# Early-fusion layer: the tokenizer's last wave in another order, with the mixer's first gated products between its norms

## The chip, the cores and the metric

The kernel runs on one core of one Trainium2 chip. The metric is the time of one execution on the device in microseconds (us), as the median of three runs.

## What is computed

Three parts follow one another on a batch of 32 images. The tokenizer makes 49 tokens of 192 channels from each image; a row for the class and 32 text rows are added, which gives 82 rows an image. Then come a Mamba mixer with a selective scan and a feed-forward part, and last attention with a mixture of eight experts. The change touches the end of the tokenizer and the start of the mixer:

```python
h = relu(dwconv(h, f1_dw, f1_pw, f1_pwb))
h = relu(dwconv(h, f2_dw, f2_pw, f2_pwb))
h = dwconv(loc + h, f3_dw, f3_pw, f3_pwb)          # 3x3 taps per channel, then a 1x1 product
t = (t - mu) / sqrt(var + 1e-05) * ln_g + ln_b     # over the 192 channels of each token
h = concatenate([cls_tok, t]), then the text rows
# mixer, for rounds of 4 images
z = (rmsnorm(layernorm(h)) @ W_in.T) * sigmoid(... @ W_gate.T)
xdbl = z @ W_xproj.T                                # dt_in, B, C
h_t = exp(dt * A) * h_{t-1} + dt * z * B            # the scan, 16 states
```

## The kernel before

**The tokenizer** (`tokenizer`) works on four chunks (CH) of eight images (IM) and runs them through a pipeline of seven waves (WAVES, w = 0 to 6). Each engine has its instructions in an order written out by hand, and semaphores join them. Chunk c goes through the convolutions in wave c, the first fusion layer (tile PF[0], DF[0]) in wave c+1, the second (PF[1], DF[1]) in wave c+2 and the third (PF[2], DF[2]) in wave c+3. The nine taps of a depthwise layer are shared: for one half of the channels VectorE multiplies and adds them (`dw`, L174 and L176, one input and the running sum in PSUM bank 3, the last tap writes DF); for the other half ScalarE weighs them (`weigh`, L344) and GpSimd adds them (`add_up`, L492).

The last 1x1 product turns the channels to the free side: TensorE makes for each two images one product in a bank of PSUM (L300; four matmuls of 192 columns, each recorded as two passes), four such for each chunk. VectorE adds the bias while it copies them to T0 (`take_rows`, L414, which raises s_t0), makes statistics of the rows (L420, L423), GpSimd makes the root (`roots`, L479 and L481), and VectorE norms the rows (`norm_rows`: eight scalings, L429, and two operations on all, L432 and L434, which raises s_t1). SyncE then stores the chunk to H, and loads weights of the mixer between the stores.

Since DF[2] is there once, the taps of a chunk wait for the products of the chunk before (s_f[2]). Since three banks are there for the products, product n waits for the add of product n-3 (s_t0). In the last wave VectorE's order is: norms of chunk 1, adds and statistics of chunk 2, taps of chunk 3, adds and statistics of chunk 3, norms of chunk 2, norms of chunk 3.

**The mixer** (`mamba`) works in eight rounds (ROUNDS) of four images, each with 16 turns, one for each state. What a round needs ahead of its scan is made in the round before it, by `pre(j, par, s, other)` of each engine. For round 0 these pieces are made in the tokenizer's last waves, at named points, where `tok` calls back `tail(point)` of the mixer: s = 0 is the scaled input hn (ScalarE, L899), s = 2 the transposes (TensorE L764, ScalarE L904), s = 3, 4, 5 the three tiles of gate and input products (TensorE L784, tanh on ScalarE L909, z on VectorE L1030), s = 6 the projection to dt, B and C (TensorE L792; ScalarE L913 to L916 copy it; VectorE takes the residual R, L1035). Two banks of PSUM (SIDE) are shared by these pieces in turn, so the products of a tile wait for z of the tile before. From there ScalarE makes softplus, which gives dt (VectorE L1038 to L1045 in round 0).

At its last but one tail VectorE halves the gate weights (L1105) and spreads the one-hot rows to sel (L1106); both raise s_cst. After the tokenizer VectorE makes `chunk_stats` of chunks 1 to 3 (L1014 to L1021), from which GpSimd makes roots (L1133, L1135), then P (L1141) and Bx (L1173), which the first scan of VectorE (L1082) needs.

Of the kernel before, what the change touches and what calls it, by code (L numbers as in the profile page):

```python
# [93 lines left out]
def tokenizer(nc, ctx, at, ps, H, vec, ident, eye, xcol, w_pl, w_pg, had, pw_mix, w96, vecs, pwb_row, lng_row, lnb_row, cls_row, txt):  # L94


    if True:
# [37 lines left out]
        f3_bank = [psC[0:PATCHES, 0, 0:2 * D], psC[0:PATCHES, 1, 0:2 * D], psC[0:PATCHES, 2, 0:2 * D]]  # L135
# [73 lines left out]
        def tensor(pe, tail):  # L209
# [32 lines left out]
            for w in range(WAVES):  # L242
# [46 lines left out]
                if 0 <= w - 3 < CH:  # L289
# [5 lines left out]
                    for n in range(c * IM // 2, (c + 1) * IM // 2):  # L295
                        if n >= 3:
                            pe.wait_ge(s_t0, n - 2)
                        for j in range(2):
                            for k in range(2):
                                mm = pe.matmul(f3_bank[n % 3][:, j * D:(j + 1) * D], dense(DF[2], k)[:, 2 * n + j - c * IM, :],  # L300
                                               wf[:, 3, k, :], start=k == 0, stop=k == 1)
                        mm.then_inc(s_f[2], 1)

        def scalar(act, tail):
# [42 lines left out]
            for w in range(WAVES):  # L347
                if w + 1 < CH:
                    gelu(w + 1)
                if w == WAVES - 1:  # L350
                    tail("last wave")
# [48 lines left out]
        def vector(v, tail):  # L400
# [9 lines left out]
            def take_rows(c):  # L410

                for n in range(c * IM // 2, (c + 1) * IM // 2):
                    v.wait_ge(s_f[2], n + 1)
                    v.tensor_tensor(T0[:, 2 * n:2 * n + 2, :], f3_bank[n % 3].rearrange("p (j c) -> p j c", j=2),  # L414
# [22 lines left out]
            for w in range(WAVES):  # L437
# [5 lines left out]
                if 0 <= w - 1 < CH:  # L443
# [3 lines left out]
                    dw(v, own, PF[0], DF[0], (0,), w - 1, V_F_DW, s_dwf[0])  # L447
                if 0 <= w - 5:
# [3 lines left out]
                if w == WAVES - 1:  # L452
                    tail("last taps")
# [7 lines left out]
                if 0 <= w - 3 < CH:  # L461
# [5 lines left out]
            take_rows(CH - 1)  # L467
            norm_rows(CH - 2)
            tail("last rows")
            norm_rows(CH - 1)  # L470
# [133 lines left out]
def mamba(nc, ctx, block, at, ps, tok, H, vec, ident, w_zg, w_x, w_dt, a_log, w_o, w_ug, w_dn, onehot, b_d, xs):  # L604
# [4 lines left out]
    if True:  # L609
# [13 lines left out]
        s_w = sem("b_w"); s_wA = sem("b_wA"); s_wo = sem("b_wo"); s_wug = sem("b_wug"); s_cst = sem("b_cst"); s_zero = sem("b_zs"); s_zf = sem("b_zf")  # L623
# [118 lines left out]
        def _(pe):  # L742
# [101 lines left out]
            def first():  # L844
                pe.wait_ge(tok.s_t0, CH * IM // 2)
                pe.sem_inc(s_left, 1)
                pe.wait_ge(s_cst, 3)
# [21 lines left out]
            EARLY = (2, 3, 4)  # L869
# [9 lines left out]
        def _(act):  # L879
# [6 lines left out]
            def softplus_in(j, m):  # L886
                if isinstance(j, int) and j == 0 and m == 0:
                    act.wait_ge(s_cst, 2)
# [89 lines left out]
            def first():  # L978
# [6 lines left out]
                act.wait_ge(s_cst, 3)  # L985
# [10 lines left out]
            def tail(point):  # L996
                pre(0, 0, 0, None)
# [5 lines left out]
        def _(v):  # L1003
# [96 lines left out]
            def tail(point):  # L1100
                if point == "last but one taps":
                    v.wait_ge(tok.s_cls, 32)
                    chunk_stats(0)
                    v.wait_ge(s_w, 64)
                    v.tensor_scalar(wzg[:, :, 0, :], wzg[:, :, 0, :], 0.5, None, ALU.mult).then_inc(s_cst, 1)  # L1105
                    v.tensor_copy(sel[:], oh[:, STATE:2 * STATE].rearrange("p (s a) -> p s a", a=1).broadcast_to([HD, STATE, 128])).then_inc(s_cst, 1)  # L1106
                if point == "last wave":
                    v.wait_ge(tok.s_lr, CH)
                    pre(0, 0, 3, None)
                if point == "last taps":  # L1110
# [994 lines left out]
```

## Time and profile before

| | us |
|---|---|
| median of 3 runs (lowest, highest) | 1568.92 (1567.16, 1569.36) |
| the profiled execution | 1572.95 |
| its span | 1571.1 |

The profile is of one execution. Engines are called PE (TensorE), PEld (its weight loads), DVE (VectorE), ACT (ScalarE), POOL (GpSimd) and SP or SPq (SyncE); DVEq is VectorE's queue, without a data instruction. A timeline has a line for each run of equal instructions: its start, how long it took in all, the instruction, and in square brackets how long the engine stood idle ahead of it and who released it. L numbers are lines of the kernel.

### The profile page before, as it was taken

The numbers are of one execution on the slowest core, as the hardware profiler recorded it, in microseconds if no ns is written. First come the engines' busy times: TensorE is split into PE (matmuls) and PEld (weight loads), VectorE is DVE, ScalarE is ACT, GpSimd is POOL, SyncE is SP. The second block draws the span as 40 slices with busy tenths as digits, with TensorE's granted clock in tenths as the row PEclk, the third lists the DMA queues.
The fourth block names the chain that finished last, engine by engine and source line by source line (L and its number), as shares of the span: only waits on it lengthen the run. The fifth ranks groups of instructions, "written<-read, shape, count | busy, mean of one in ns | idle before, by whom it ended". The sixth has DMA issues, their size and how long they took to land. (4 is left out here: it accounts for less than half of the span.)

```text
span 1571.1 us, 19634 instructions
## 1 busy us (share of the span) xinstructions
PE 1263.1 (80%) x5818; PEld 832.9 (53%) x5819; DVE 1044.7 (66%) x1955; ACT 708.8 (45%) x1486; POOL 755.3 (48%) x493
## 2 busy tenths in 40 slices
PE   6796736388898989889878589888888439999996
PEld 4342323144554555545435368777777417777775
DVE  3699787899888978989895437766667503333332
ACT  1147522576757758585752055444442112222221
POOL 2028963668758675776771501144444622222222
PEclk9696667699999999999999789999897569999999
DMA  5100000530403304040300111112100122222221
GB/s 158 52 1 0 27 9 26 164 129 1 129 17 113 103 26 129 0 129 6 123 1 0 36 54 40 54 53 67 51 22 22 29 55 35 37 37 37 34 36 23
DMA packets 71417, 81.02 MB, mean 52 GB/s; under 512 B 13390, under 2 KB 63205, under 8 KB 71257
## 3 DMA queue, kind: packets, MB, share of 16 engines
q1 hardware_dynamic: 52066, 68.63, 14.0%
q0 software_dynamic: 17152, 9.24, 4.3%
q10 hardware_dynamic: 2136, 2.37, 0.5%
q8 instruction: 32, 0.52, 0.1%
q14 instruction: 31, 0.25, 0.1%
HBM read 48.86 MB, written 30.01 MB: 50 GB/s over the span
## 5 line engine op out<-in xcount | busy, mean ns | idle before, releaser
L1173 POOL TENSOR_TENSOR Bx<-dtz,Bb 128x984 f32<-128x984 f32 x128 | 288.2, 2270 | 54.3 <-DVE hs L1082 54.3
L1082 DVE TENSOR_TENSOR_SCAN hs<-ps,Bx 128x492 f32<-128x492 f32 x256 | 287.6, 1164 | 30.4 <-ACT ps L973 25.4
L973 ACT ACTIVATE ps<-dt,A 128x324 f32<-128x324 f32 (+1 forms) x512 | 214.1, 454 | 106.5 <-DVE hs L1082 104.9
L856 PE MATMUL ps<-hs,b_id 128*128 128x492 f32 x512 | 243.3, 598 | 9.2 <-DVE y L1050 9.1
L1937 POOL DMA_INDIRECT out<-yt,dest x48 | 74.4, 1549 | 219.9 <-DVE yt L1924 214.7
L1092 DVE TENSOR_TENSOR hs<-hs,ps 128x984 f32<-128x984 f32 x128 | 150.2, 1174 | 2.6
L1818 PE MATMUL e_ps<-W,xT 97*128 (+1 forms) x384 | 138.3, 503 | 1.5 <-ACT xT L1872 1.0
L856 PEld LDWEIGHTS ps<-hs,b_id 128*128 128x128 f32 x512 | 94.4, 198 | 84.5 <-issue 82.3
L1910 DVE COPY hT_<-e_ps 128x768 f32<-128x768 f32 x48 | 46.0, 958 | 129.0 <-PE e_ps L1827 128.7
L1722 POOL TENSOR_TENSOR c_x<-c_x,bro 82x192 f32<-82x192 f32 x32 | 19.7, 616 | 195.2 <-DVE c_x L1565 194.7
L1837 PE MATMUL e_ps<-W,hT_ 128*128 x576 | 109.2, 327 | 0.8 <-DVE yb L1918 0.8
L1878 ACT ACTIVATE hb<-e_ps 128x768 f32<-128x768 f32 x48 | 38.9, 811 | 144.1 <-PE e_ps L1818 144.1
L823 PE MATMUL ps<-hfT,wug 96*128 96x328 f32 x256 | 83.7, 472 | 24.8 <-DVE av L1067 24.1
L1713 POOL DMA_INDIRECT buckets<-XS,c_slot x64 | 91.1, 1424 | 24.9 <-issue 19.1
L1818 PEld LDWEIGHTS e_ps<-W,xT 97*128 97x128 f32 (+1 forms) x384 | 69.9, 192 | 55.0 <-issue 17.0
L1837 PEld LDWEIGHTS e_ps<-W,hT_ 128*128 128x128 f32 x576 | 91.4, 190 | 1.4 <-issue 1.4
L492 POOL TENSOR_TENSOR DF<-DF,prod 96x441 f32<-96x441 f32 x84 | 87.5, 1042 | 6.6
L841 PE MATMUL ps<-P,sel 96*128 96x328 bf16 x128 | 40.2, 316 | 54.8 <-DVE hs L1092 41.0
L823 PEld LDWEIGHTS ps<-hfT,wug 96*128 96x128 f32 x256 | 49.1, 199 | 64.0 <-DVE av L1067 40.7
L1419 PEld LDWEIGHTS c_ps<-V,PT 82*82 82x82 f32 x768 | 69.3, 169 | 13.8 <-issue 7.6
L1872 ACT ACTIVATE xT<-e_ps,m_vec 96x128 f32<-96x128 f32 x96 | 38.4, 448 | 81.5 <-PE e_ps L1808 81.5
L1532 DVE TENSOR_REDUCE mx<-c_ps 82x12 f32<-82x984 f32 x32 | 37.7, 1177 | 51.7 <-PE c_ps L1406 51.4
(247 smaller groups left out, 2446.4 us busy)
## 6 DMA issues: line engine op xcount, KB each, us to landing
Bb<-b_rows SPq DMA_DIRECT2D x32, 656.0 KB, 6.6
buckets<-b_zero SPq DMA_DIRECT2D x8, 2288.0 KB, 15.4
xg<-buckets SPq DMA_DIRECT2D x48, 104.0 KB, 1.9
xc<-in_xcol SPq DMA_DIRECT2D x4, 1176.0 KB, 9.4
W<-in_w1d SPq DMA_DIRECT2D x8, 582.0 KB
W<-in_w2d SPq DMA_DIRECT2D x8, 576.0 KB
out<-H SPq DMA_DIRECT2D x8, 246.0 KB
H<-P SPq DMA_DIRECT2D x4, 294.0 KB
```

The source lines that it names most:

```text
L492: g.tensor_tensor(out, a, prod[:, (9 * n + t) % PRODUCTS], ALU.add).then_inc(s_sum, 1)
L823: mm = pe.matmul(ps[:, bank(name), 0:N], wug[:, k, w_, m * 128:(m + 1) * 128], hfT[:, k, :], start=k == 0, stop=k == 1)
L856: mm = pe.matmul(ps[:, BANK_Y + h, 0:HALF], ident[:], f2(hs[:, s % LONG])[:, h * HALF:(h + 1) * HALF], start=s == 0, stop=s == STATE - 1)
L973: a = act.activation(ps[:, BANK_A + h, c:c + w].rearrange("p (g t) -> p g t", t=S)[:, :, 1:S], dt[:, (par + t // STATE) % 2, m, g0 * S:g1 ...
L1082: v.tensor_tensor_scan(f2(hs[:, t % LONG])[:, c], ps[:, BANK_A + h, 0:HALF], f2(Bx[:, t % RING])[:, c], 0.0, ALU.mult, ALU.add).then_inc(s ...
L1092: v.tensor_tensor(hs[:, s % LONG], hs[:, s % LONG], ps[:, BANK_C + s % 2, 0:N].rearrange("p (a n) -> p a n", a=1).broadcast_to([128, NI, N ...
L1173: g.tensor_tensor(Bx[:, t % RING], dtz[:, p], Bb[:, p, t % STATE, :].rearrange("p (a n) -> p a n", a=1).broadcast_to([128, NI, N]), ALU.mu ...
L1419: mm = pe.matmul(ps[0:S, HEAD_OUT + c % 2, h * (DH + 1):(h + 1) * (DH + 1)], PT[:, c % 2, h, :], V[:, vpar, c, h, :], start=True, stop=True)
L1713: g.indirect_dma_start(out=xs, out_offset=bass.IndirectOffsetOnAxis(ap=slot[:, par, k, c:c + 1], axis=0), in_=XS[:, par, c, :], in_offset= ...
L1818: mm = pe.matmul(ps[:, 1 + 2 * p + h, 0:384], xT[c_, p, k, :], W1[c_, k, bass.ds(e, 1), h * 384:(h + 1) * 384].rearrange("p a n -> p (a n) ...
L1837: mm = pe.matmul(ps[:, 7, 0:D], hT[:, p, k, :], W2[:, k, bass.ds(e, 1), :].rearrange("p a n -> p (a n)"), start=k == 0, stop=k == KF - 1)
L1937: g.indirect_dma_start(out=out, out_offset=bass.IndirectOffsetOnAxis(ap=dest[:, p:p + 1], axis=0), in_=yt[:, p, :], in_offset=None, comput ...
```

## The change

VectorE's order in the last wave becomes: taps of chunk 3, adds and statistics of chunk 2, norms of chunk 1, norms of chunk 2, adds and statistics of chunk 3, norms of chunk 3. The pieces of z go to other places: the first behind the adds of chunk 2 as before, the second behind the statistics, the third between the norms of chunks 1 and 2, R behind the norms of chunk 2. TensorE makes all pieces up to the projection (s = 6) ahead of the products of chunk 3. From product 8 on the products have four banks, 0, 1, 2 and 4. Halving the gate weights and making sel move from VectorE to ScalarE, ahead of what it weighs in wave 5. The memset of the pads raises a semaphore of its own.

```diff
-        f3_bank = [psC[0:PATCHES, 0, 0:2 * D], psC[0:PATCHES, 1, 0:2 * D], psC[0:PATCHES, 2, 0:2 * D]]
+        BANK_OF = [n % 3 if n < CH * IM // 4 else (0, 1, 2, 4)[n % 4] for n in range(CH * IM // 2)]
+        f3_bank = [ps[0:PATCHES, k, 0:2 * D] for k in BANK_OF]
...
                     for n in range(c * IM // 2, (c + 1) * IM // 2):
-                        if n >= 3:
-                            pe.wait_ge(s_t0, n - 2)
+                        if BANK_OF[n] in BANK_OF[:n]:
+                            pe.wait_ge(s_t0, max(k for k in range(n) if BANK_OF[k] == BANK_OF[n]) + 1)
+                        elif BANK_OF[n] == 4:
+                            pe.wait_ge(s_r2, CH)
...
-                if w == WAVES - 1:
-                    tail("last wave")
+                if w >= WAVES - 2:
+                    tail("last wave" if w == WAVES - 1 else "last but one wave")
...
+                if w == WAVES - 1:
+                    break
                 if 0 <= w - 5:
                     norm_rows(w - 5)
                 if 0 <= w - 4:
                     take_rows(w - 4)
-                if w == WAVES - 1:
-                    tail("last taps")
...
-                if 0 <= w - 3 < CH:
+                if 0 <= w - 3 < CH - 1:
...
-            take_rows(CH - 1)
+            v.wait_ge(s_lr, CH)
+            v.wait_ge(s_f[2], (CH - 1) * IM // 2)
+            dw(v, own, PF[2], DF[2], (0,), CH - 1, V_F_DW + 36, s_dwf[2])
+            take_rows(CH - 2)
+            tail("rows taken")
+            norm_rows(CH - 3)
+            tail("rows normed")
             norm_rows(CH - 2)
             tail("last rows")
+            take_rows(CH - 1)
+            tail("all rows taken")
             norm_rows(CH - 1)
...
-                pe.wait_ge(s_cst, 3)
+                pe.wait_ge(s_cst, 2)
...
-            EARLY = (2, 3, 4)
+            EARLY = (2, 3, 4, 5, 6)
...
-                if isinstance(j, int) and j == 0 and m == 0:
-                    act.wait_ge(s_cst, 2)
...
-                act.wait_ge(s_cst, 3)
+                act.wait_ge(s_pads, 1)
...
-                pre(0, 0, 0, None)
+                if point == "last but one wave":
+                    act.wait_ge(s_w, 64)
+                    act.activation(wzg[:, :, 0, :], wzg[:, :, 0, :], ACT.Copy, scale=0.5).then_inc(s_cst, 1)
+                    act.activation(sel[:], oh[:, STATE:2 * STATE].rearrange("p (s a) -> p s a", a=1).broadcast_to([HD, STATE, 128]),
+                                   ACT.Copy).then_inc(s_cst, 1)
+                if point == "last wave":
+                    pre(0, 0, 0, None)
...
                     chunk_stats(0)
-                    v.wait_ge(s_w, 64)
-                    v.tensor_scalar(wzg[:, :, 0, :], wzg[:, :, 0, :], 0.5, None, ALU.mult).then_inc(s_cst, 1)
-                    v.tensor_copy(sel[:], oh[:, STATE:2 * STATE].rearrange("p (s a) -> p s a", a=1).broadcast_to([HD, STATE, 128])).then_inc(s_cst, 1)
                 if point == "last wave":
-                    v.wait_ge(tok.s_lr, CH)
                     pre(0, 0, 3, None)
-                if point == "last taps":
+                if point == "rows taken":
                     pre(0, 0, 4, None)
+                if point == "rows normed":
+                    pre(0, 0, 5, None)
                 if point == "last rows":
+                    pre(0, 0, 6, None)
+                if point == "all rows taken":
                     v.wait_ge(tok.s_t0, CH * IM // 2)
-                    v.memset(ps[:, BANK_A:BANK_A + 2, :], 0.0).then_inc(s_cst, 1)
-                    pre(0, 0, 5, None)
+                    v.memset(ps[:, BANK_A:BANK_A + 2, :], 0.0).then_inc(s_pads, 1)
...
-            pre(0, 0, 6, None)
```

VectorE, from the end of `chunk_stats(0)` in wave 5 on. PF_61 is PF[2], P_58 is T0. Before:

```order
L1105 TENSOR_SCALAR wzg<-wzg 96x2x384
L1106 CAST sel<-oh 96x2048
L174 TENSOR_SCALAR ps<-PF_61,vec 96x441
L176 SCALAR_TENSOR_TENSOR ps<-PF_61,vec,ps 96x441 x7
L176 SCALAR_TENSOR_TENSOR DF_65<-PF_61,vec,ps 96x441
L429 TENSOR_SCALAR P_58<-P_58,mv,rs 49x192 x8
L432 TENSOR_TENSOR P_58<-P_58,rows 49x1536
L434 TENSOR_TENSOR P_58<-P_58,rows 49x1536
L414 TENSOR_TENSOR P_58<-ps,rows 49x384 x4
L1030 SCALAR_TENSOR_TENSOR z<-sg,ps 128x328
L420 BN_STATS st<-P_58 49x6 x8
L423 BN_AGGR mv<-st 49x2 x8
```

With the change:

```order
L175 TENSOR_SCALAR ps<-PF_61,vec 96x441
L177 SCALAR_TENSOR_TENSOR ps<-PF_61,vec,ps 96x441 x7
L177 SCALAR_TENSOR_TENSOR DF_65<-PF_61,vec,ps 96x441
L175 TENSOR_SCALAR ps<-PF_61,vec 96x441
L177 SCALAR_TENSOR_TENSOR ps<-PF_61,vec,ps 96x441 x7
L177 SCALAR_TENSOR_TENSOR DF_65<-PF_61,vec,ps 96x441
L417 TENSOR_TENSOR P_58<-ps,rows 49x384 x4
L1045 SCALAR_TENSOR_TENSOR z<-sg,ps 128x328
L423 BN_STATS st<-P_58 49x6 x8
L426 BN_AGGR mv<-st 49x2 x8
L1045 SCALAR_TENSOR_TENSOR z<-sg,ps 128x328
L432 TENSOR_SCALAR P_58<-P_58,mv,rs 49x192 x8
```

The two instructions on wzg and sel are gone, the taps of the last chunk (the second L175) stand right behind those of chunk 2, and the norms (L432 to L437) stand behind adds, z and statistics.

TensorE, from the products of chunk 2 (L300, with the change L303) to the step sizes. Before:

```order
L300 MATMUL ps<-wf,DF_65 49x192 x16
L764 MATMUL ps<-b_id,hn 96x82 x8
L784 MATMUL ps<-hT,wzg 128x328 x8
L300 MATMUL ps<-wf,DF_65 49x192 x16
L784 MATMUL ps<-hT,wzg 128x328 x4
L792 MATMUL ps<-z,wx 96x328 x6
L770 MATMUL ps<-dtin,wdt 128x328 x3
```

With the change:

```order
L303 MATMUL ps<-wf,DF_65 49x192 x16
L775 MATMUL ps<-b_id,hn 96x82 x8
L795 MATMUL ps<-hT,wzg 128x328 x12
L803 MATMUL ps<-z,wx 96x328 x6
L303 MATMUL ps<-wf,DF_65 49x192 x16
L781 MATMUL ps<-dtin,wdt 128x328 x3
```

The third tile of gate products (L784, now L795) and the projection (L792, now L803) stand ahead of the products of chunk 3.

## Rows read from the trace of the kernel before

**Rows 1.** Page of the kernel before, its first line

```profile
span 1571.1 us, 19634 instructions
```

**Rows 2.** Timeline of VectorE, 296 to 306 us; the first line names the columns

```profile
start us, us, engine line op out<-in xcount [idle before <-releaser]
...
296.79 0.20 DVE L1021 TENSOR_SCALAR b_negm<-b_mv 82x8 f32<-82x8 f32 x1
297.55 1.18 DVE L1038 TENSOR_TENSOR ax<-u,ax 128x984 f32<-128x984 f32 x1 [0.56 <-ACT ax L933]
...
305.37 2.25 DVE L1082 TENSOR_TENSOR_SCAN hs<-ps,Bx 128x492 f32<-128x492 f32 x2 [2.98 <-POOL Bx L1173]
```

**Rows 3.** Timeline of GpSimd, 297 to 304 us

```profile
297.12 2.90 POOL L1133 TENSOR_TENSOR b_root<-b_root,b_nh 82x16 f32<-82x16 f32 x1 [0.16 <-DVEq L1023]
300.10 1.15 POOL L1135 TENSOR_TENSOR b_nb<-b_root,b_negm 82x16 f32<-82x16 f32 x1
...
303.01 8.92 POOL L1173 TENSOR_TENSOR Bx<-dtz,Bb 128x984 f32<-128x984 f32 x4
```

**Rows 4.** Timeline of VectorE, 231 to 257 us

```profile
231.72 0.56 DVE L1105 TENSOR_SCALAR wzg<-wzg 96x768 f32<-96x768 f32 x1 [0.16 <-DVE b_negm L1021]
232.19 1.22 DVE L1106 CAST sel<-oh 96x2048 bf16<-96x2048 f32 x1
233.33 0.67 DVE L174 TENSOR_SCALAR ps<-PF,vec 96x441 f32<-96x441 f32 x1
...
239.85 2.40 DVE L429 TENSOR_SCALAR P<-P,mv,rs 49x192 f32<-49x192 f32 x8 [0.16 <-DVE DF L176]
...
252.43 0.50 DVE L1030 SCALAR_TENSOR_TENSOR z<-sg,ps 128x328 f32<-128x328 f32 x1 [3.52 <-PE ps L784]
...
255.98 0.67 DVE L174 TENSOR_SCALAR ps<-PF,vec 96x441 f32<-96x441 f32 x1
```

**Rows 5.** Timeline of VectorE, 265 to 287 us

```profile
265.29 0.55 DVE L414 TENSOR_TENSOR P<-ps,rows 49x384 f32<-49x384 f32 x1 [2.95 <-PE ps L300]
...
269.94 0.55 DVE L414 TENSOR_TENSOR P<-ps,rows 49x384 f32<-49x384 f32 x1 [0.75 <-PE ps L300]
270.52 2.17 DVE L420 BATCH_NORM_STATS2 st<-P 49x6 f32<-49x192 f32 x8
...
280.66 2.38 DVE L429 TENSOR_SCALAR P<-P,mv,rs 49x192 f32<-49x192 f32 x8
...
286.54 0.48 DVE L1035 TENSOR_TENSOR R<-ps,P 64x328 f32<-64x328 f32 x1
```

**Rows 6.** Timeline of TensorE, 239 to 286 us

```profile
239.81 8.52 PE L300 MATMUL ps<-wf,DF 96*49 96x192 f32 x32 [6.58 <-DVEq L180]
...
252.98 2.47 PE L784 MATMUL ps<-hT,wzg 96*128 96x328 f32 x8 [0.70 <-DVE z L1030]
262.45 7.46 PE L300 MATMUL ps<-wf,DF 96*49 96x192 f32 x32 [7.00 <-DVEq L180]
...
280.88 4.92 PE L792 MATMUL ps<-z,wx 128*96 128x328 f32 x12 [8.57 <-DVE z L1030]
```

**Rows 7.** Busy time by stretch: stretch and length, engines, then TensorE's granted clock, DMA share, GB/s

```profile
240.00:246.00 6.00, 6.00 (x20) 3.86 (x20) 5.93 (x11) 6.00 (x13) 0.00 (x0) 0.50 0.00 0
267.00:270.00 3.00, 3.00 (x19) 2.13 (x18) 1.16 (x3) 0.00 (x0) 0.00 (x0) 1.00 0.00 0
```

**Rows 8.** Timeline of ScalarE, 233 and 296 us

```profile
233.26 1.06 ACT L396 ACTIVATE R<-ps,vec 96x392 f32<-96x392 f32 x2 [25.10 <-PE ps L237]
...
295.59 1.02 ACT L931 ACTIVATE lnw<-u 128x984 f32<-128x984 f32 x1
```

**Rows 9.** Timeline of GpSimd, 249 and 274 us

```profile
249.44 7.80 POOL L492 TENSOR_TENSOR DF<-DF,prod 96x441 f32<-96x441 f32 x7
...
273.80 1.71 POOL L481 TENSOR_TENSOR rs<-ve,nh 49x8 f32<-49x8 f32 x1
```

**Rows 10.** Timeline of VectorE, 196 to 216 us, the scalings of norm_rows(0)

```profile
201.12 9.52 DVE L429 TENSOR_SCALAR P<-P,mv,rs 49x192 f32<-49x192 f32 x8 [4.24 <-POOL rs L481]
```

More of the change, by code:

```diff
@@ L295, in tensor @@
                     for n in range(c * IM // 2, (c + 1) * IM // 2):
-                        if n >= 3:
-                            pe.wait_ge(s_t0, n - 2)
+                        if BANK_OF[n] in BANK_OF[:n]:
+                            pe.wait_ge(s_t0, max(k for k in range(n) if BANK_OF[k] == BANK_OF[n]) + 1)
+                        elif BANK_OF[n] == 4:
+                            pe.wait_ge(s_r2, CH)
                         for j in range(2):
                             for k in range(2):
-                                mm = pe.matmul(f3_bank[n % 3][:, j * D:(j + 1) * D], dense(DF[2], k)[:, 2 * n + j - c * IM, :],
+                                mm = pe.matmul(f3_bank[n][:, j * D:(j + 1) * D], dense(DF[2], k)[:, 2 * n + j - c * IM, :],
                                                wf[:, 3, k, :], start=k == 0, stop=k == 1)
@@ L413, in take_rows @@
                     v.wait_ge(s_f[2], n + 1)
-                    v.tensor_tensor(T0[:, 2 * n:2 * n + 2, :], f3_bank[n % 3].rearrange("p (j c) -> p j c", j=2),
+                    v.tensor_tensor(T0[:, 2 * n:2 * n + 2, :], f3_bank[n].rearrange("p (j c) -> p j c", j=2),
                                     rows[:, 0:1, :].broadcast_to([PATCHES, 2, D]), ALU.add).then_inc(s_t0, 1)
@@ L622, in mamba @@
         zero = sb("b_zero", [128, RW])
-        s_w = sem("b_w"); s_wA = sem("b_wA"); s_wo = sem("b_wo"); s_wug = sem("b_wug"); s_cst = sem("b_cst"); s_zero = sem("b_zs"); s_zf = sem("b_zf")
+        s_w = sem("b_w"); s_wA = sem("b_wA"); s_wo = sem("b_wo"); s_wug = sem("b_wug"); s_cst = sem("b_cst"); s_pads = sem("b_pads"); s_zero = sem("b_zs"); s_zf = sem("b_zf")
         s_own = sem("b_own"); s_left = sem("b_left"); s_var = sem("b_var"); s_root = sem("b_roots"); s_nh = sem("b_nhs"); nh = sb("b_nh", [S, 2, IM])
```

## The prediction

> **What bounds the kernel now.** I read the page first for the span [rows 1], then the timelines of VectorE, GpSimd and TensorE around the end of the tokenizer, because the change touches nothing behind it. The first scan of the mixer's rounds starts at 305.37 [rows 2]; all that follows keeps its instructions and its order, so a shift of that start should reach the end one for one.
>
> What releases this scan? It waited 2.98 us for GpSimd's Bx [rows 2]. GpSimd had come to Bx through a queue: root of the last chunk at 297.12, b_nb at 300.10, a memset and the residual P, and Bx at 303.01 [rows 3]. The root at 297.12 waits for `chunk_stats(3)`, which VectorE ends with the negm that starts at 296.79 [rows 2]. So the end of VectorE's queue of the tokenizer sets the start of the rounds. ScalarE's softplus chain is nearly as late (VectorE waited 0.56 us for it at 297.55 [rows 2]), but GpSimd's queue covers that. **A microsecond is won only where VectorE idles less, or works less, before 297.**
>
> VectorE has three pieces of idle time there: 3.52 us for z of the first tile [rows 4], and then the last products: 2.95, 1.51 and two of 0.75 us in front of the four adds, of which the first and the last are shown [rows 5]. Everything else between 228 and 297 is work.
>
> The products are the key. A group of four takes 8.52 us at 239.81 and 7.46 us at 262.45 on TensorE [rows 6]. The granted clock tells why: 0.50 in 240:246, that is 1.2 GHz, and 1.00 in 267:270, 2.4 GHz [rows 7]; TensorE had stood still for 6.58 and 7.00 us before them [rows 6]. In the second group the first product took 2.84 us (262.45 to the add at 265.29) and the last 1.3 us (the wait of 0.75 and the add of 0.55 ahead of it). In both groups the time is that of the clock, and not that of a bank: the bank that the fourth product needs is free by the add at 265.29. **So four banks in place of three are worth nothing by themselves.** They are needed, however: with three, the fourth product of chunk 2 would wait for an add that now stands behind taps, which wait for that product.
>
> **The change, part by part**, on the clock of the trace of before.
>
> *Halved gate weights and sel to ScalarE.* VectorE loses 0.56 and 1.22 us, in all 1.6 between 231.72 and 233.33 [rows 4]. ScalarE makes 984 elements in 1.02 us [rows 8], so 768 and 2048 take an estimated 2.9 us. It does them ahead of the weighing at wave 5, after which it idles 25.10 us [rows 8]; what it weighs there feeds GpSimd's add-ups, which take 1.1 us each (7.80 for seven [rows 9]) and are waited for only 16 us after they end. Cost 0. If that cover were gone, it would be at most 2.9 us.
>
> *Last taps first.* The taps of chunk 2 run 231.75 to 238.1 (6.4 us, from 233.33 to 239.85 less a gap [rows 4]). Its products start at 238.2. The last taps overwrite DF, so they wait for all four products. Before, `norm_rows(1)` (from 239.85) lay beside the products [rows 4]; now nothing does. I take 8.0 us, between 8.52 and 7.46 [rows 6], as TensorE again comes from a pause (5 us): products end at 246.2. Bounds: 5.2 us (all at 1.3) and 11.4 us (all at 2.84); the rows say neither. **VectorE waits 8.1 us here, a new wait.** The last taps run 246.3 to 252.65 instead of from 255.98 [rows 4]. GpSimd's add-ups, behind the same products, end near 255, and TensorE needs them only at 271.
>
> *Adds, z0, stats.* Four adds without a pause, 2.0 us; z0, 0.4, for which the old wait of 3.52 is gone (transposes and gate products have had 6 us); stats and aggregates 2.8 (270.52 to 273.29 [rows 5]): VectorE is free at 258.0.
>
> *z1.* Its two products start only after z0, at 255.25, since the two banks for them are shared. At the pace of 252.98 they take 2.47 us [rows 6] and nothing is late; TensorE had paused for 0.70 there. But now TensorE has stood still for 5 us before them, as before the cold groups. Cold I take 4.4 us: 0.55 for each of eight, the pace of the first half of the x-projection (its first output is read 3.3 us after 280.88, six passes [rows 6]). Then z1 starts at 259.65 and **VectorE waits 1.7 us**. Bounds 0 and 2.2.
>
> *Norms and gated product.* `norm_rows(1)` takes 5.9 (280.66 to 286.54 [rows 5]) until 266.0; z2 until 266.4. `norm_rows(2)` and R follow until 272.7. The x-projection, which lay at 280.88, starts at 266.45: 4.92 us [rows 6], to 271.4. It now stands ahead of the last products on TensorE's queue: with them at 1.3 us each, these end at 276.6. Bounds: 8.5 us for both (warm from the start) and 11.8 (projection all cold, 6.6); I take 10.1, since TensorE's pause ahead of z2 is again 2 to 4 us.
>
> *Last adds and norm.* VectorE stands at the adds from 272.7 and follows TensorE: last add over at 277.25 (0.55). **That is about 2.4 us of waiting**, in place of 6. Stats to 280.05; the memset of the pads hides in GpSimd's root, which takes 2.2 us from the last aggregate (its pow 1.71 from 273.80, the aggregate over at 273.3 [rows 5, 9]). `norm_rows(3)` has no other norm ahead of it now that covers the root, and starts at 282.35, where it was 280.66 [rows 5]: 1.7 later. R (0.41) is no longer behind it: the rest of VectorE's queue is 1.3 later.
>
> *The handover.* VectorE's dt chain needs no ScalarE any more and starts 0.5 us sooner after negm. GpSimd's b_nb took 1.15 us at 300.10 beside it, and P followed until 303.01 [rows 3]; part of this shifts away: I take 0.4 us, bounds 0 and 0.7.
>
> *SyncE.* The loads of A, wo and wdn stand behind the store of chunk 1, now at 266; A is read at 288. Bs is ready 14 us sooner, but its broadcast stands behind the last store, as before. Cost 0.
>
> **Sum:** +1.3 - 0.4 = +0.9 us, on 1572.95 us of the profiled execution. That execution is 4.0 above the median of 1568.92, which is what I predict against: 1568.92 + 0.9 = **1569.8 us**. A measurement of this kernel can tell about 0.2%, 3.1 us, from no change: this is no change.
>
> **The rivals.**
>
> *The clock comes up sooner (faster).* The products take 7.2, the pair for z1 is warm (1.7), projection and products take 8.5 (1.6 less): 0.8 + 1.7 + 1.6 = 4.1 us better, 1565.7 us. For it: TensorE has shorter pauses than before. Against: pauses of 6.58 and 7.00 us ended cold both times. Chance 0.11.
>
> *It stays low longer (slower).* 9.0 us for the products, 4.8 for the pair, 11.8 at the end: 1.0 + 0.4 + 1.7 = 3.1 more, 1572.9 us. For it: the group at 239.81 was at 1.2 GHz through 240:246 [rows 7]. Chance 0.09. The Trainium skill ("TensorE: Matmul & The Clock Gate", What's actually happening) says that the throttled clock is the default and that activity releases it; the cold starts in these rows agree, and by that rule every new pause of TensorE is paid here.
>
> *Norms beside GpSimd's add-ups (slower).* `norm_rows(0)` took 9.52 us for its eight scalings while GpSimd added [rows 10]; at 280.66 they take 2.4. If GpSimd's add-ups ran into `norm_rows(1)`, this would be 7.1 us more, z2 and all behind it as late: 1577 us. It decides once the add-ups end after 260. They take 8.9 us (7.80 for seven of eight [rows 9]) and start with the last taps, so they end near 255: 5 us to spare. Chance 0.04. The Trainium skill ("GPSIMD Engine Reference", Key points) states that GpSimd shares its SBUF interfaces with VectorE and contends with two-port modes or two SBUF inputs; the 9.52 agrees. By it the last taps, with one input in PSUM, are safe beside the add-ups.
>
> *The change doesn't do what it says.* If the order of z pieces among norms mattered, the 3.52 us would be gain. They are gone, but the new wait of 8.1 swallows them. That is in the forecast, and so is its chance.
>
> **How the numbers follow.** Forecast 0.76 (within 0.2%: 1565.8 to 1572.0), faster 0.11, slower 0.13. Range: down to 1566.2 and up to 1573.0, most of both clock cases and a microsecond of spread between runs (1567.16 to 1569.36).
>
> **What would show it.** In the new profile: VectorE idle about 8 us ahead of the last taps, released by the products (wrong if under 6.5); its wait ahead of z1 1 to 2 us; no wait ahead of z0; waits of about 2.4 us in all at the last adds; 1 to 1.5 us ahead of the last norm; the first scan at 306.2 against 305.37. The forecast is wrong if the first scan comes before 303 or after 309, or if a different engine releases the last `chunk_stats`.

## The result, and the profile after

The changed kernel takes **1585.68 us** (median of 6 runs, 1583.75 to 1593.13), against 1569.30 for the kernel before in the same comparison (6 runs, 1567.16 to 1571.61). The ratio is 1.0113, with a 95% interval of 1.0089 to 1.0137. That is 16 us slower, where no change was forecast. The profiled execution is one of the longer ones, 1590.27 us.

The first line of the page of the changed kernel, against [rows 1]:

```profile
span 1588.5 us, 19633 instructions
```

The end of the tokenizer came out nearly as the sum had it. Timeline of VectorE of the changed kernel, 246 to 307 us, which answers to [rows 2, 4, 5]:

```profile
246.00 0.68 DVE L175 TENSOR_SCALAR ps<-PF,vec 96x441 f32<-96x441 f32 x1 [7.80 <-PE ps L303]
...
254.39 0.47 DVE L1045 SCALAR_TENSOR_TENSOR z<-sg,ps 128x328 f32<-128x328 f32 x1
...
259.77 0.50 DVE L1045 SCALAR_TENSOR_TENSOR z<-sg,ps 128x328 f32<-128x328 f32 x1 [2.15 <-PE ps L795]
...
273.37 0.55 DVE L417 TENSOR_TENSOR P<-ps,rows 49x384 f32<-49x384 f32 x1 [0.52 <-PE ps L303]
...
277.27 0.55 DVE L417 TENSOR_TENSOR P<-ps,rows 49x384 f32<-49x384 f32 x1 [0.75 <-PE ps L303]
...
282.77 2.40 DVE L432 TENSOR_SCALAR P<-P,mv,rs 49x192 f32<-49x192 f32 x8 [0.96 <-POOL rs L492]
...
298.50 0.19 DVE L1036 TENSOR_SCALAR b_negm<-b_mv 82x8 f32<-82x8 f32 x1
...
306.72 2.25 DVE L1097 TENSOR_TENSOR_SCAN hs<-ps,Bx 128x492 f32<-128x492 f32 x2 [2.98 <-POOL Bx L1186]
```

And the timeline of TensorE, 238 to 272 us, against [rows 6]:

```profile
238.31 7.59 PE L303 MATMUL ps<-wf,DF 96*49 96x192 f32 x32 [5.07 <-DVEq L181]
...
254.92 4.74 PE L795 MATMUL ps<-hT,wzg 96*128 96x328 f32 x8 [5.08 <-DVE z L1045]
...
266.70 5.20 PE L803 MATMUL ps<-z,wx 128*96 128x328 f32 x12 [1.64 <-DVE z L1045]
```

The new wait ahead of the last taps is 7.80 us, z0 waits for nothing, z1 waits 2.15, the last adds wait 0.52 and three times 0.75, and the last norm waits 0.96 for its root. The first scan starts at 306.72, 1.35 us after that of [rows 2]. The two traces can be compared so directly, because the last instruction of `chunk_stats(0)`, just ahead of what the change touches, starts at the same time in both; before, then after:

```profile
231.40 0.16 DVE L1021 TENSOR_SCALAR b_negm<-b_mv 82x8 f32<-82x8 f32 x1
```
```profile
231.40 0.16 DVE L1036 TENSOR_SCALAR b_negm<-b_mv 82x8 f32<-82x8 f32 x1
```

**The other 15 us arise behind it, in code that the change does not touch.** From the first scan to the last H it is 575.0 us before (305.37 to 880.34) and 590.6 us after (306.72 to 897.29). The groups of VectorE in this stretch show which waits grew. Before, 305.3 to 880.9 us (busy time, mean in ns, then the idle time ahead and who ended it):

```profile
L1092 DVE TENSOR_TENSOR hs<-hs,ps 128x984 f32<-128x984 f32 x128 | 150.2, 1174 | 2.6
L1067 DVE SCALAR_TENSOR_TENSOR av<-th,ps 128x328 f32<-128x328 f32 x32 | 15.9, 496 | 3.9 <-PE ps L823 3.0
...
L1072 DVE TENSOR_TENSOR H<-x,ps 82x384 f32 (+1 forms) x16 | 8.8, 547 | 20.3 <-PE ps L833 20.3
L1059 DVE TENSOR_TENSOR x<-xl,ps 82x384 f32<-82x384 f32 x16 | 8.6, 542 | 6.8 <-PE ps L810 6.8
```

After, 306.6 to 897.9 us:

```profile
L1107 DVE TENSOR_TENSOR hs<-hs,ps 128x984 f32<-128x984 f32 x128 | 150.2, 1174 | 6.7 <-issue 4.0 <-DVE hs L1097 0.5
L1082 DVE SCALAR_TENSOR_TENSOR av<-th,ps 128x328 f32<-128x328 f32 x32 | 15.9, 496 | 5.6 <-PE ps L834 4.8
...
L1074 DVE TENSOR_TENSOR x<-xl,ps 82x384 f32<-82x384 f32 x16 | 8.8, 549 | 13.7 <-PE ps L821 13.4
L1087 DVE TENSOR_TENSOR H<-x,ps 82x384 f32 (+1 forms) x16 | 8.8, 548 | 21.8 <-PE ps L844 21.8
```

The work is the same to a tenth. The waits are not: 4.1 us more at the products with C, 4.0 of them "issue" (the engine waited for nothing that the profile shows), and 6.9 more for the output products of TensorE, with 1.7 and 1.5 for av and H.

The "issue" idle has two places, 142 us apart, which is two rounds: one pass of the loop. Timeline of VectorE after:

```profile
513.08 1.18 DVE L1107 TENSOR_TENSOR hs<-hs,ps 128x984 f32<-128x984 f32 x1 [2.03 <-issue]
...
654.62 1.18 DVE L1107 TENSOR_TENSOR hs<-hs,ps 128x984 f32<-128x984 f32 x1 [2.00 <-issue]
```

These are the first products with C of the second and third pass, behind the loop's jumps. The end of a round, where VectorE makes y of the last products with C and TensorE begins the output products, is called the drain here. TensorE at a drain, before (timeline, then granted clock, the third number from the right):

```profile
509.17 0.31 PE L841 MATMUL ps<-P,sel 96*128 96x328 bf16 x1 [1.50 <-DVE hs L1092]
510.78 1.89 PE L856 MATMUL ps<-hs,b_id 128*128 128x492 f32 x4 [1.30 <-DVE y L1050]
```
```profile
511.00:514.00 3.00, 3.00 (x14) 1.98 (x14) 2.97 (x4) 1.70 (x4) 1.12 (x1) 1.00 0.00 0
```

The same drain after:

```profile
514.32 0.31 PE L852 MATMUL ps<-P,sel 96*128 96x328 bf16 x1 [3.41 <-DVE hs L1107]
515.93 3.54 PE L867 MATMUL ps<-hs,b_id 128*128 128x492 f32 x4 [1.30 <-DVE y L1065]
```
```profile
516.00:519.00 3.00, 3.00 (x4) 1.34 (x5) 2.96 (x3) 1.70 (x4) 0.97 (x1) 0.50 0.00 0
```

TensorE's pause grew from 1.50 to 3.41 us; the granted clock behind it is 0.50 (1.2 GHz) where it was 1.00, the same products take 3.54 us and not 1.89, and VectorE then waits 1.40 us for the output products. Measured from drain to drain (the start of the first y of each), the rounds take 69.7, 70.1, 69.7, 70.1, 68.4, 68.3 us before and 71.2, 71.9, 70.0, 71.6, 73.6, 71.2 after. 68.3 us is a round in which the clock stays up, as e12 and e13 below show.

One more view answers to the "issue": the DMA queues, where queue 14 loads instructions; before, then after.

```profile
q14 instruction: 31, 0.25, 0.1%
```
```profile
q14 instruction: 41, 0.34, 0.1%
```

### The profile page after: what moved, and what is told of

Its sections match the earlier page's. It is cut to its first block and busy times, and to the rows that moved or that the text cites. A ratio compares the mean times of both kernels' runs of the same rounds, so it can differ in the third digit from the quotient of the medians.

```text
span 1588.5 us, 19633 instructions
## 1 busy us (share of the span) xinstructions
PE 1275.0 (80%) x5818; PEld 839.0 (53%) x5819; DVE 1044.5 (66%) x1953; ACT 710.3 (45%) x1488; POOL 754.1 (47%) x493
## 5 line engine op out<-in xcount | busy, mean ns | idle before, releaser
L867 PE MATMUL ps<-hs,b_id 128*128 128x492 f32 x512 | 249.7, 612 | 9.0 <-DVE y L1065 9.0
```

The costliest lines, as they stand in the source:

```text
L867: mm = pe.matmul(ps[:, BANK_Y + h, 0:HALF], ident[:], f2(hs[:, s % LONG])[:, h * HALF:(h + 1) * HALF], start=s == 0, stop=s == STATE - 1)
```

## The experiments

Theory A: wzg and sel were two of VectorE's instructions ahead of the loop. In its stream of the built program (numbered from 0, waits and branches counted) the loop of 343 instructions begins at 577 before and at 575 after, and the change moved it across a border of code loading; the longer pauses pull TensorE's clock down. Theory B: the later start alone moves the rounds against the clock's decisions. Theory C: the new order itself costs.

All results in one table. "First scan", "rounds" (first scan to last H) and "rest" (the run's time less the start of the last H) are of the one profiled execution; "x" is VectorE's wait for output products in the rounds.

| run | median us | ratio to before, 95% | first scan | rounds | rest | x |
|---|---|---|---|---|---|---|
| before | 1566.9 to 1570.4 | | 305.4 | 575.0 | 692.6 | 6.8 |
| changed | 1585.7 | 1.0089 to 1.0137 | 306.7 | 590.6 | 693.0 | 13.7 |
| e1 fillers | 1569.1 | 0.9984 to 1.0013 | 302.6 | 573.7 | 689.6 | 6.8 |
| e2 order alone | 1574.3 | 1.0027 to 1.0065 | 304.1 | 576.8 | 689.6 | 8.4 |
| e3 moved alone | 1586.8 | 1.0064 to 1.0143 | 304.5 | 599.8 | 689.1 | 17.0 |
| e4 pause at head | 1583.8 | 1.0069 to 1.0117 | 302.2 | 596.0 | 689.6 | 14.3 |
| e5 200 memsets | 1569.9 | 0.9990 to 1.0022 | 302.3 | 575.5 | 693.2 | 6.8 |
| e6 100 memsets | 1572.2 | 0.9986 to 1.0021 | 304.5 | 575.0 | 694.7 | 6.8 |
| e10 125 memsets | 1583.9 | 1.0069 to 1.0152 | 301.4 | 585.6 | 692.9 | 11.4 |
| e7 pause in the middle | 1592.1 | 1.0126 to 1.0155 | 304.1 | 591.9 | 694.7 | 9.8 |
| e16 one pause | 1573.0 | 1.0031 to 1.0060 | 302.0 | 578.9 | 689.0 | 8.2 |
| e8 busy drain, changed | 1584.3 | 1.0076 to 1.0112 | 306.0 | 583.8 | 692.9 | 3.7 |
| e9 busy drain, filled | 1568.5 | 0.9979 to 1.0018 | 303.8 | 577.1 | 692.9 | 3.7 |
| e11 both pauses, changed | 1577.0 | 1.0029 to 1.0061 | 302.8 | 580.9 | 692.4 | 4.9 |
| e12 both pauses, filled | 1574.3 | 1.0005 to 1.0030 | 304.8 | 577.6 | 692.5 | 3.7 |
| e13 and the end, filled | 1559.8 | 0.9944 to 0.9969 | 304.2 | 566.4 | 689.6 | 3.7 |
| e14 and the end, changed | 1570.7 | 1.0017 to 1.0038 | 303.4 | 572.1 | 690.9 | 4.8 |
| e15 and the end, before | 1564.2 | 0.9975 to 0.9998 | 303.2 | 566.3 | 694.6 | 3.7 |

Two columns warn against reading one pair of traces. The first scan of the kernel before and of e4, e7 and e16, which are the same program up to the loop, starts at 302.0 to 305.4; the rest takes 689 to 695 us where nothing in it was changed. The first spread lies ahead of the last wave: from the instruction at 231.40 shown above (at 227.3 to 231.5 in the other traces) to the first scan it is 73.97 to 74.12 us in all eight traces with VectorE's old order and wzg and sel on it. The rounds and this stretch are the clean measures.

**Is it the place of the code, the start or the order?** Three runs.

```diff
 # e1: the changed kernel, in VectorE's tail at "last but one taps"
+for k in range(2):
+    n = own.did(v.memset(negm[:, B - 1 - k:B - k], 0.0))
 # e2: the changed kernel; wzg and sel back on VectorE at their old place
 # e3: the kernel before; wzg and sel on ScalarE as in the change, nothing else
```

> The changed kernel with two memsets of one column each on VectorE at the place (last but one taps) where the two instructions for wzg and sel had stood, so that VectorE's loop of the rounds begins after as many instructions as in the kernel before. Theory A (place of the code): the two pauses of 2.0 us in front of the first scan product of a pass (513.08 and 654.62) and the one of 0.49 at the loop's entry are instruction loads, which come because the loop's body lies two instructions earlier in VectorE's stream; they go, the TensorE pauses that they lengthen go too, and the kernel takes 1570 to 1573 us. Theory B (the start): the first scan at 306.7 in place of 305.4 alone shifts the rounds against the chip's clock decisions; the pauses of 2.0 us may go or stay, and the time stays at 1580 or more. Theory C (the order): the new order of the last wave costs in a way that reaches into the rounds; 1580 or more, with the pauses.

> The changed kernel, but wzg and sel stay on VectorE at their old place: the new order alone. Theory A: VectorE's stream ahead of the loop is as long as before, so no pause of 2.0 us at a pass; the last taps start no later for it, since the new wait for the products covers or shifts by the 1.7 us of the two; 1570 to 1574 us. Theories B and C: 1582 or more.

> The kernel before with wzg and sel on ScalarE and nothing else: the old order, VectorE's stream two instructions shorter ahead of the loop. Theory A: the pauses of 2.0 us at 513 and 654 appear as in the changed kernel, and it takes 1578 to 1590 us although its first scan is no later than before. Theory B: the first scan comes 0 to 1.6 us sooner, no pauses of their own; 1560 to 1572 us. Theory C: 1567 to 1570 us.

Two memsets of one column each bring 16 us back: 1569.1 us, a microsecond under what was expected, the "issue" pauses gone, queue 14 again with 31 packets. The new order with the loop at 577 takes 1574.3 us, just above what was expected, and has no such pause. The old order with the loop at 575 has all of the loss, 1586.8 us, though its first scan is at 304.5. VectorE of e3:

```profile
514.96 1.18 DVE L1098 TENSOR_TENSOR hs<-hs,ps 128x984 f32<-128x984 f32 x1 [2.28 <-issue]
...
661.64 1.18 DVE L1098 TENSOR_TENSOR hs<-hs,ps 128x984 f32<-128x984 f32 x1 [2.11 <-issue]
```

So the order and the start are cleared of the 16 us; the two instructions that left VectorE are the cause, and not what they do, since memsets replace them. Theories B and C fall. The order is not free: with wzg and sel on VectorE, e2 is 0.27 to 0.65% above the kernel before.

**Where is the border?** The kernel before with k memsets of one element on VectorE while it waits for its first taps:

```diff
+for k in range(200):                       # e5; 100 in e6, 125 in e10
+    i = own.did(v.memset(DF[2][:, 0, k % 64, k // 64:k // 64 + 1], 0.0))
+own.need(i)
```

> The kernel before with 200 memsets of one element each (and one wait) on VectorE at the start, in its idle time of 15.7 us before the first taps: the loop's body begins 201 instructions later in VectorE's stream, the order and the work of the last wave are untouched. The body has 343 instructions. Theory A, in the form that the code is loaded in pieces of 256 instructions of which two are kept (so says the page on the launch of the runtime of the Trainium skill): beginning at a piece's first or second instruction the body lies in two pieces (before, and with the two fillers), two instructions earlier it touches three (changed), and 201 later it touches three again: pauses of about 2 us at the second and third pass, more packets in the queue of instructions (41 and not 31), 1580 to 1590 us. Rival A2 (only the jump onto the last instructions of a piece costs, whatever the number of pieces) and Theory B: no such pause, 1567 to 1572 us, at most 3 us more if the memsets outlast the idle time.

The stated form of theory A was wrong here: no pause, 1569.9 us. But the run shows two things. Its memsets, 27 ns each, outran the code; timeline of VectorE of e5:

```profile
14.12 4.76 DVE L408 MEMSET DF<- 96x1 f32 x175
20.42 0.73 DVE L408 MEMSET DF<- 96x1 f32 x25 [1.53 <-issue]
```

The first memset is instruction 17 of the stream, so it stood still at 17 + 175 = 192. And the queue of instructions did load more, without a pause:

```profile
q14 instruction: 42, 0.34, 0.1%
```

0.25 MB in 31 packets is 8 KB a packet. At 64 bytes an instruction (a size taken from the Trainium skill, "Runtime: NRT & Kernel Launch", Instruction fetch mechanics: 16 KiB hold 256) that is 128 instructions, and borders at 192 + 128 n are at 576 and 704: before, the loop begins one instruction behind the border, after, one instruction ahead of it.

> The kernel before with 125 memsets of one element (and one wait) on VectorE at the start: its loop of the rounds begins 126 instructions later, at 703 of its stream where the kernel before has 577, the changed one 575 and the run with 200 memsets 778. In that run the memsets stood still for 1.53 us after the 175th, instruction 192 of the stream, and the queue of instructions moved 0.25 MB in 31 packets, 8 KB or 128 instructions each. So the pieces end at 192, 320, ..., 576, 704, ... Theory A3 (a jump to the last instruction or two of a piece needs two loads in a row, of which VectorE's queue hides one): 703 is the last instruction of a piece, as 575 is; the pauses of 2.0 us are back at the second and third pass although the stream is 126 longer and not 2 shorter, 1578 to 1592 us. Rival (pieces of 256, ends at 448 and 704 only): 703 stalls as well, but then 575 should not have, so the two together are shown by no such rule. Rival (any jump whose body lies in four pieces and not three is lucky or not for another reason): no pause, 1567 to 1573 us.

> The same with 100 memsets: the loop begins at 678, with 26 instructions left in its piece; its body lies in four pieces, as with 200 memsets (54 left) and in the changed kernel (1 left). Theory A3: the queue of instructions loads more (41 or 42 packets), and the pause is hidden or short, since 26 instructions take VectorE more time than the second load: 1567 to 1573 us. Rival (every loop in four pieces stalls unless far from the end): pauses of 1 to 2 us, 1578 to 1590 us.

Both as theory A3 had them. At 703, the last instruction ahead of the next border, the pauses are back, in the kernel before with nothing moved to ScalarE and with the earliest first scan of all, 301.4; timeline of VectorE of e10:

```profile
506.55 1.18 DVE L1095 TENSOR_TENSOR hs<-hs,ps 128x984 f32<-128x984 f32 x1 [2.21 <-issue]
...
649.54 1.18 DVE L1095 TENSOR_TENSOR hs<-hs,ps 128x984 f32<-128x984 f32 x1 [1.90 <-issue]
```

At 678 there are 42 packets too and no pause. So the starts 577 (3 pieces of 128 touched, 31 packets), 678 and 778 (4 pieces, 42 packets) run through, and 575 and 703 (4 pieces, 41 and 42 packets, one instruction left in the first) stop for 2 us at each jump. That a jump to the end of a piece needs two loads in a row, one of which VectorE's queued scans cover, fits all five; the loads themselves cannot be seen one by one, so this is the likely mechanism and not shown. The same page of the Trainium skill, in the same section, states that a taken branch out of the two pages at hand stalls for the fetch. The traces agree that jumps can stall, but not with its pages of 256 instructions: laid so that 575 stalls and 577 does not, these would have 778 (e5) stall and 703 (e10) run through, and both came out the other way.

**Why 16 us and not 4.5?** First, a pause made by work.

```diff
 # e4: VectorE, at the head of each of the three passes; e7: ahead of the ninth state
 # of the pass's first round; e16: once, ahead of the loop
+for k in range(4):
+    v.bn_stats(st[:, k, :], f2(wdn)[0:S, 0:512])
```

> The kernel before with four statistics of 512 columns each (estimated 0.5 to 0.7 us each) on VectorE at the head of each of the loop's three passes, into a tile that nobody reads any more: a pause of some 2.3 us for the scans, made by work and not by an instruction load. Theory A: each costs more than itself, since TensorE stands still for as long and its clock falls afterwards: 3 x 2.3 = 7 us direct and 3 to 12 us from the clock, 1579 to 1590 us, with more drains where VectorE waits 1.4 us for the output products. Rival (the pause is only itself): 1576 us.

> The kernel before with the same four statistics of 512 columns as in the run with the pause at the head of the pass (2.5 us by its trace, three times), but ahead of the ninth state of the pass's first round, where TensorE has products of the gated MLP and no drain stands next. Theory A with the clock as the rest: the pause costs itself, 3 x 2.5 = 7.5 us, and little from the clock, 1574 to 1578 us, against 1583.8 at the head. Rival (a pause anywhere lowers the clock as far ahead of the drains, or GpSimd and ScalarE cover it): 1581 or more, or under 1572.

> The kernel before with the four statistics of 512 columns (2.5 us) once, ahead of the loop, with no change in the loop. If the rounds find back to their good length of 68.3 us after a single pause, as they do after their first rounds in the kernel before, it costs 2 to 5 us: 1571 to 1575 us. Rival (one pause is enough to move all rounds into the bad pattern of 71.2 us): 1585 or more.

One such pause takes 2.44 us; timeline of VectorE of e4:

```profile
364.84 2.44 DVE L1122 BATCH_NORM_STATS2 b_st<-wdn 82x6 f32<-82x512 f32 x4
```

Three of them are 7.3 us. At the head of the pass they cost 16 to 21 us (1583.8 against 1568.1 in the same comparison, rounds of 596.0 against 575.0): more than themselves, as expected. In the middle I had expected 7.5 us, and they cost 17 to 22 (1592.1 against 1570.2). So it is not the drain next door alone: up to the last drain VectorE's waits for TensorE grew by 3.0 us at the output products, 3.4 at av and 2.1 at H. The single pause costs 4 to 6 us, and the rounds find back to 68.4 us in the third and fourth round after it (71.2, 70.1, 68.4, 68.4, 69.7, 70.0), where e4 has 70.0, 71.8, 73.4, 73.4, 73.4, 71.2. That pauses in every pass leave no time to find back is how I read it; no run varies their distance.

Then the other way round: give TensorE work in its pauses.

```diff
 # e8 (changed kernel), e9 (with the fillers of e1): PE
+def busy(cols):
+    for k in range(2):
+        pe.matmul(ps[:, bank("O0"), 0:cols], ident[:], f2(wdn)[:, 0:cols], start=True, stop=True)
 ...
+if s == 0: free("O0", p, other); busy(360)   # in post, ahead of the first C product
+if s == 0 and not (isinstance(i, int) and i == 0): busy(300)   # in step, behind spread_c
 # e11, e12: and in post at s == 12, but for the last round, zeros added to y
+for k in range(6):
+    pe.matmul(ps[:, BANK_Y + k % 2, 0:RW], ident[:], zero[:], start=False, stop=False)
 # e13 (filled), e14 (changed), e15 (kernel before): and in the last post, s in 7, 10..14
+for k in range(4 if s == 7 else 1):
+    cols = HALF if s == 7 else 256
+    pe.matmul(ps[:, BANK_Y + k % 2, 0:cols], ident[:], f2(wdn)[:, 0:cols], start=True, stop=True)
```

> The changed kernel with four added products on TensorE in each round, where it stands still at the drain (two of 360 columns ahead of the first C product, two of 300 behind it, into the bank that the output products overwrite): the pauses of VectorE at the loop's jumps stay, TensorE's are filled. If the clock makes the rest of the loss: the waits of 1.40 us for the output products go in all rounds, the kernel keeps 2 x 2.0 + 0.5 us of the loss, 1571 to 1576 us. If the clock is only a companion: 1583 or more.

> The same added products in the changed kernel with the two fillers on VectorE: no pauses at the jumps, TensorE's filled. Where the kernel before has two rounds with a wait of 1.40 us for output products and its neighbours, these go: 1563 to 1567 us, 2 to 5 us below the kernel before. Rival (the added products delay the C product and y's own products by as much as they win): 1568 to 1573 us.

By their numbers both go to the rival. VectorE's wait for output products fell to 3.7 us in both, yet 1584.3 and 1568.5 us are the times without the added products. There is a second pause in each round, 3.11 us ahead of the third pair of the MLP's products, and the clock fell behind that one; e9, two stretches, the granted clock third from the right:

```profile
486.00:489.00 3.00, 2.23 (x4) 1.50 (x5) 2.97 (x5) 0.68 (x2) 3.00 (x2) 0.50 0.00 0
489.00:492.00 3.00, 3.00 (x7) 1.75 (x6) 1.74 (x3) 2.65 (x7) 3.00 (x2) 0.50 0.00 0
```

> The changed kernel with added products in both places where TensorE stands still in a round: at the drain, as in the run before with added products, and six of 208 columns of zeros, added to y, ahead of the third pair of products of the gated MLP, where TensorE waits 3.11 us for av. The pauses of VectorE at the jumps stay (2.0, 2.0 and 0.5 us). If what is left of the loss is TensorE's clock after such pauses, the rounds are 68.3 us long plus the pauses: first scan to last H 569 to 575 us in the trace (590.6 in the changed kernel), 1568 to 1574 us. Rival (the clock falls all the same, or the added products cost what they save): 1580 or more.

> The same added products in the changed kernel with the two fillers on VectorE (no pauses at the jumps). Theory: all rounds 68.3 us, first scan to last H 568 to 571 us (573.7 with fillers alone), 1563 to 1567 us, faster than the kernel before. Rival: 1568 to 1573 us.

With both pauses busy, e12 has no low clock from 357 to 852 us and rounds of 68.3 and 68.4 us throughout; e11 has them too, but for 70.1 and 70.3 with a jump in each and 69.6 behind the second. The changed kernel gains 9 us by it, though 1577.0 us and rounds of 580.9 lie above what was expected. But e12 got slower than e1, against the forecast. All of that lies behind the last drain, 41.0 us where the kernel before has 33.9; TensorE there, timelines of e12 and e13, each with the granted clock of a stretch behind:

```profile
853.11 4.74 PE L844 MATMUL ps<-hfT,wug 96*128 96x328 f32 x8 [0.62 <-ACT hfT L980]
858.52 4.74 PE L844 MATMUL ps<-hfT,wug 96*128 96x328 f32 x8 [0.67 <-DVE av L1095]
```
```profile
863.00:868.00 5.00, 4.34 (x9) 2.52 (x8) 0.99 (x2) 0.44 (x1) 0.00 (x0) 0.50 0.00 0
```
```profile
852.49 2.47 PE L848 MATMUL ps<-hfT,wug 96*128 96x328 f32 x8 [0.29 <-ACT hfT L984]
...
855.63 2.47 PE L848 MATMUL ps<-hfT,wug 96*128 96x328 f32 x8 [0.23 <-DVE av L1099]
```
```profile
863.00:868.00 5.00, 4.68 (x25) 3.70 (x25) 0.99 (x2) 0.44 (x1) 0.00 (x0) 1.00 0.02 3
```

> The changed kernel with the two fillers and the products added in both pauses of a round, and now also in the last round's MLP behind the last drain, where TensorE waits 4.33 us for hf and 0.6 to 0.8 us ahead of each pair (four of 492 columns, then one of 256 ahead of each group, into y's banks, which are free there). If the low clock of that stretch (pairs of 4.74 us, 41 us from the last drain to the last H against 34) comes from those pauses, its pairs take 2.5 us and the stretch 28 to 33 us: 1560 to 1566 us, faster than both kernels. Rival (the added products come in the way of the pairs, or the clock stays low): 1568 to 1575 us.

> The same in the changed kernel without the fillers. Theory (the rest of the loss is TensorE's clock, and these products hold it up): 4 to 5 us above the run with fillers, the 2.0 + 2.0 + 0.5 us of the jumps and no more. Rival (something else follows from the jumps): 10 us or more above it.

> The same added products in the kernel before: old order, wzg and sel on VectorE, the loop at 577. By the forecast's sum the new order costs 0.9 us, so this is within 2 us of the run with fillers and the new order. Rival (the new order is worth something that the clock's jitter hides): 3 us or more slower than it.

With this stretch busy too, e13 takes **1559.8 us, 0.44% less than the kernel before** (0.31 to 0.56) and by the medians 1.6% less than the changed one; all six rounds take 68.3 to 68.4 us and the stretch at the end 29.7. It beats both kernels. Without the fillers (e14) the same kernel takes 10.9 us more by the medians, 6.3 by the profiled pair, where I had said 4 to 5; by the medians that is the rival's number. Its rounds take 572.1 us against 566.4, 5.7 more: 4.5 us of jumps, 0.5 at the loop's entry, and one drain with a low clock behind the second jump. The other 5 us of the medians are in no trace that I have. The kernel before with these products (e15) takes 1564.2 us, 4.4 more than e13, outside the 2 us that were expected. But its rounds are equal (566.3), its first scan is 1.0 us sooner and its rest 5.0 us longer, in code that is alike. That rest differs by TensorE's clock too. From VectorE's first list of slots for the experts (tile c_slot) to its first sum of H and XN, e13 and e15, with TensorE's busy time right behind the length and the granted clock third from the right:

```profile
1005.44:1238.42 232.98, 191.13 (x1467) 162.17 (x1465) 155.04 (x480) 83.55 (x153) 103.73 (x86) 0.82 0.15 40
```
```profile
1002.04:1242.53 240.49, 199.24 (x1467) 169.52 (x1465) 155.35 (x479) 83.77 (x153) 103.67 (x86) 0.79 0.15 39
```

The 1467 products are the same, and they take 8.1 us more at the lower clock.

## Why the prediction was wrong

- **The step that failed** is its first: "all that follows keeps its instructions and its order, so a shift of that start should reach the end one for one". The instructions are the same; their place in VectorE's stream is not. The part on wzg and sel priced what the two instructions take ("Cost 0" on ScalarE, 1.6 us saved on VectorE) and not that they stood ahead of a loop. What the runs showed in its place: two instructions fewer put the loop's start at 575, VectorE stops for 2.0 us at each of two jumps and 0.5 at the loop's entry, and TensorE's clock falls behind the longer pauses, 15.6 us in the rounds by the first pair of traces. No rival held this mechanism, and 1585.7 lies 12.7 us above the range. With two memsets in their place the forecast's 1569.8 meets a measured 1569.1.
- Of the 16.9 us between the rounds of the changed and the filled kernel, 4.5 are the pauses at jumps and entry, by their rows. The rest went when TensorE's pauses were filled: from the first scan to the last drain the two then differ by 5.4 us (e11, e12) and 5.7 (e14, e13), of which 1.2 each time is a wait at the drain behind the second jump, where the clock had fallen to 0.66 (645:650). So by the traces about 11 us more were TensorE's clock. The medians are less clear: e11 and e12 differ by 2.7 us, with an end that is 2.0 us shorter in e11, and e14 and e13 by 10.9.
- That a new pause of TensorE is paid was weighed for the tokenizer alone. In the rounds, where the prediction had looked at nothing, it was paid as well, though not each time: the first jump of e11 brought no low clock.
- The tokenizer, step by step: wait ahead of the last taps 7.80 (forecast 8.1, at 246.3, came at 246.00); z0 none; the pair for z1 4.74 us and a wait of 2.15 (4.4 and 1.7); the x-projection at 266.70 (266.45); waits at the last adds 2.77 (2.4); the last norm at 282.77 (282.35); the first scan at 306.72 (306.2). Each was right to about half a microsecond, with 0.96 us of waiting ahead of the last norm where 1 to 1.5 were said. This part of the mechanism was right.
- The sum, +0.9 us, was short by about half a microsecond. From the last instruction of `chunk_stats(0)` to the first scan it is 73.97 to 74.12 us in eight traces of the old order (before, e4, e5, e6, e7, e10, e15, e16) and 75.32 to 75.84 in eight of the new one (changed, e1, e8, e9, e11 to e14): 1.5 us more in the mean, 1.35 in the first pair. The first scan by itself, from the start of the span, would not have told it: 301.4 to 305.4 against 302.6 to 306.7.
- "Four banks in place of three are worth nothing by themselves" was not tried alone. ScalarE's two instructions cost nothing visible. What they save VectorE was forecast at 1.6 us. In the stretch up to the first scan it is 1.0 in the old order (e3, 72.97 against 73.97 before) and 0.9 in the new one (e1, 75.36 against 76.26 for e2). By the medians e2 is 5 us above e1; the pair of traces puts 3.1 of it into the rounds, in which both kernels do the same. That this is the clock is not shown.

**Left open:** why the same code behind the rounds gets a mean clock of 0.82 in some runs and 0.81 or 0.79 in others. The stretch of e13 and e15 above takes 232.8 to 233.0 us in e1, e3, e13 and e16, 235.9 to 236.6 in the kernel before, the changed one, e7 and e14, and 240.5 in e15, and most of the spread of "rest" lies there. Open too is where 5 of the 10.9 us between e14 and e13 are.

## What to carry to other kernels

When a change adds or removes instructions ahead of a loop, count where the loop now begins in the engine's stream (only VectorE was tried here), and look in the first profile for "issue" idle at the head of a pass. More packets in the instruction queue are a hint and no proof, since e5 and e6 had 42 and no pause. Here a filler of two instructions was the whole repair. Where a kernel's rounds hang on a pause of TensorE, price a new pause by what the clock does after it, and measure the stretch in question over several traces, from a row just ahead of it, since start and rest move by 3 to 5 us by themselves. If the clock falls behind regular pauses, small products into a free bank can hold it up, but all of the pauses have to be filled: in the filled kernel, filling one of two gained nothing (1568.5 against 1569.1), and leaving out the end was worse (1574.3).

## What the runs showed of the hardware

- VectorE stood still for 1.53 us at instruction 192 of its stream (e5), and for 1.9 to 2.5 us at each jump back to a loop start at 575 or 703 (two rows in each of six traces: changed, e3, e8, e10, e11, e14). Jumps to 577, 678 and 778 cost nothing that can be seen. Pieces of 128 instructions (8 KB a packet) with borders at 192, 576 and 704 fit all of this, and e10 was forecast from them.
- A pause of 2.44 us of VectorE cost 5 to 7 us when repeated in each pass, at both places that were tried, and 4 to 6 us when it came once.
- Equal products behind the rounds, 1467 of them, took 191.1 us of TensorE in e13 and 199.2 in e15, at mean granted clocks of 0.82 and 0.79.
- The granted clock stayed at 0.50 through four pairs of products with pauses of only 0.62 to 0.67 us between them (e12, pairs of 4.74 us), and at 1.00 through the same four pairs once products of 256 columns stood in the gaps (e13, 2.47 us).
